# Both products of a scan step ahead of both scans, through two PSUM banks, with the attention's transposes in one bank

## What is computed

```python
# state-space layer, 256 inner channels, 16 states each
xz = einsum('blc,ec->ble', xn, W_in); xi, z = split(xz, 2)
xc = silu(conv4(xi)); dt, Bm, Cm = split(einsum('bld,ed->ble', xc, W_x))
delta = softplus(einsum('blr,dr->bld', dt, W_dt) + b_dt)
dA = exp(d_t[:, :, None] * A)
hst = hst * dA + (d_t * u_t)[:, :, None] * B_t[:, None, :]
y_t = einsum('bdn,bn->bd', hst, C_t)
out = einsum('bld,cd->blc', (y + xc * Dp) * silu(z), W_out) + x
# attention
energy = einsum('bci,bcj->bij', q, k)
out = gamma * einsum('bcj,bij->bci', v, softmax(energy)) + x
# second attention: energies of theta and phi, values x, then conv_w and batch norm, + x
```

## Time and profile before

| | |
|---|---|
| median of 3 runs | 5648.49 us (5642.84 to 5652.95) |
| the profiled execution's own time | 5654.98 us |
| its span, first to last instruction | 5653.2 us |
| mean granted clock of TensorE | 0.955 |
| VectorE busy | 5067.2 us, 90% |
| GpSimd busy | 4724.3 us, 84% |
| TensorE busy (matmuls) | 4649.7 us, 82% |
| ScalarE busy | 3709.2 us, 66% |

### The profile page before, as it was taken

One profiled execution on the slowest core, in us unless ns is written; L12 is line 12 of the kernel. 1 busy time (PEld: TensorE's weight loads), 2 busy tenths in 40 slices (PEclk: granted clock), 3 DMA queues, 4 the chain that ended last, 5 costly groups with the idle time before them and its releaser, 6 DMA issues.

```text
span 5653.2 us, 61917 instructions
## 1 busy us (share of the span) xinstructions
PE 4649.7 (82%) x17331; PEld 2705.2 (48%) x17331; DVE 5067.2 (90%) x5978; ACT 3709.2 (66%) x6077; POOL 4724.3 (84%) x3342
## 2 busy tenths in 40 slices
PE   6568888888888888888888888888888888888871
PEld 6135554455445444545444455445445544554450
DVE  4699999999999999999999999999999999999933
ACT  3456677667766766676677667766666776677633
POOL 0698999999989889898989998989889899999910
PEclk9689999999999999999999999999999999999995
DMA  4456656655655565555556665665566566656517
GB/s 132 176 224 224 224 208 223 229 222 216 224 224 215 215 225 217 216 219 225 223 207 224 224 225 217 222 220 212 219 224 223 210 221 229 224 208 224 219 74 301
DMA packets 199100, 1216.87 MB, mean 215 GB/s; under 512 B 27881, under 2 KB 28657, under 8 KB 67697
## 3 DMA queue, kind: packets, MB, share of 16 engines
q1 hardware_dynamic: 194416, 1196.26, 57.4%
q10 hardware_dynamic: 4352, 16.78, 0.7%
HBM read 1158.43 MB, written 54.53 MB: 215 GB/s over the span
## 4 chain that ended last, share of the span: by engine, by line
PE 38%; DVE 22%; ACT 14%; issue 13%; POOL 10%; DMA 1%; DVEq 0%; SPq 0%; POOLq 0%; ACTq 0%
PE psA L814 13%; PE psE L814 11%; DVE hs L488 8%; DVE psD L484 7%; PE psT L814 7%; POOL pa L300 5%; PE psT L987 4%; ACT da L680 4%; ACT p L726 3%; DVE nm L513 3%; PE psY L814 2%; POOL pa L306 2%; POOL pa L310 1%; ACT L649 1%; ACT pt L690 1%
## 5 line engine op out<-in xcount | busy, mean ns | idle before, releaser
L300 POOL TENSOR_TENSOR pa<-hs,rows_all 128x1024 f32<-128x1024 f32 x1024 | 2412.8, 2356 | 396.8 <-DVE hs L488 396.5
L680 ACT ACTIVATE da<-delta,neg_a 128x512 f32<-128x512 f32 x2048 | 1382.1, 719 | 288.3 <-DVE hs L488 276.2
L484 DVE TENSOR_TENSOR psD<-rows_all,psU 128x512 f32<-128x512 f32 x2048 | 1416.5, 692 | 84.7 <-POOL hlast L304 6.3
L306 POOL TENSOR_TENSOR pa<-pa 128x512 f32<-128x512 f32 x1024 | 1317.1, 1286 | 40.2
L488 DVE TENSOR_TENSOR_SCAN hs<-da,hlast,psD 128x512 f32<-128x512 f32 x1024 | 1310.9, 1280 | 36.3
L488 DVE TENSOR_TENSOR_SCAN hs<-da,psD 128x512 f32<-128x512 f32 x1024 | 1249.4, 1220 | 35.2
L814 PE MATMUL psA<-pt,va 128*128 128x256 f32 x4096 | 989.5, 391 | 71.2 <-DVE x L531 43.7
L814 PEld LDWEIGHTS psA<-pt,va 128*128 128x128 f32 x4096 | 770.0, 194 | 295.5 <-DVE x L531 77.1
L513 DVE TENSOR_REDUCE nm<-psE 128x1 f32<-128x1024 f32 x512 | 620.1, 1211 | 201.1 <-PE psE L814 198.8
L726 ACT ACTIVATE p<-psE,nm 128x1024 f32<-128x1024 f32 x512 | 571.5, 1116 | 316.8 <-DVE nm L513 316.7
L690 ACT ACTIVATE pt<-psT 128x512 f32<-128x512 f32 x1024 | 555.5, 596 | 304.4 <-PE psT L987 301.0
(11 more groups left out here) (186 smaller groups left out, 5017.6 us busy)
## 6 DMA issues: line engine op xcount, KB each, us to landing
rows_all<-bc_scratch SPq DMA_DIRECT2D x1024, 1024.0 KB, 4.7
xin<-x SPq DMA_DIRECT2D x40, 512.0 KB, 7.7
xres<-x SPq DMA_DIRECT2D x64, 256.0 KB, 6.1
x_scratch<-x SPq DMA_DIRECT2D x32, 512.0 KB, 4.3
f_scratch<-fa SPq DMA_DIRECT2D x32, 512.0 KB, 6.8
xres<-x SPq DMA_DIRECT2D x8, 512.0 KB, 3.6
x1g<-x SPq DMA_DIRECT2D x8, 512.0 KB, 3.7
fa<-x SPq DMA_DIRECT2D x8, 512.0 KB, 3.7
```

The lines of the kernel that those rows point to most:

```text
L300: pool.tensor_tensor(pa[:, k % PROD, :, :], hs[:, sl, :, :], rows_all[:, slot, 2:4, :], ALU.mult).then_inc(S["prod"], 1)
L306: pool.tensor_tensor(pa[:, k % PROD, 0, :], pa[:, k % PROD, 0, :], pa[:, k % PROD, 1, :], ALU.add).then_inc(S["pair"], 1)
L484: dve.tensor_tensor(psD[:, :], rows_all[:, slot, j, :], psU[:, :], ALU.mult).then_inc(S["dbu_ok"], 1)
L680: act.activation(da[:, k % 2, j, :], delta[:, h, cols(ch)], ACT.Exp, scale=neg_a[:, h, 2 * q + j:2 * q + j + 1]).then_inc(S["da_ok"], 1)
```

## The change

psD gets a second bank. psA is no longer a bank of its own: it is bank 1 of psT. What shared psT has to move:

- DVE: `scans` is split into `spread_inputs` (both products of a step, each into its own bank) and `scan_state` (one scan). A step is now: product 0, product 1, (xn), scan 0, small items, scan 1, row maximum, attended. The psU copy (`inputs`) is made in the step before it is needed, between the two scans. The waits for POOL (`prod`, `hlast_ok`) stand ahead of the first scan and not of the first product.
- PE and ACT: both halves of a tile's transposes go through bank 0 of psT; a half waits until ACT has copied the half before it. `ORDER` puts other work between the halves where there is some. The keys go through psE. The variance and both step sizes go through bank 0 (one after the other), the two gates are separate words in the order 1, 0, inner1 stands a step earlier, and the residual's first product is a word of its own.

```diff
-        psD = ps("psD", [128, CH])
+        psD = ps("psD", [128, 2, CH])
         psT = ps("psT", [128, 2, CH])
-        psA = ps("psA", [128, CH])
+        psA = psT[:, 1, :]
...
-        AT_C, AT_N, AT_X, AT_Z, AT_B, AT_P = 0, 3, (5, 7), 9, 10, 11
+        AT_C, AT_N, AT_X, AT_Z, AT_B, AT_P = 0, 3, (5, 6), 9, 10, 11
...
+                def inputs(b, k):
+                    ch, h = divmod(k // PAIRS, NH)
+                    wait(dve, "du_ok", b, k // PAIRS + 1)
+                    wait(dve, "dbu_ok", b, 2 * k)
+                    dve.tensor_copy(psU[:, :], du[:, h, cols(ch)]).then_inc(S["u_ok"], 1)
+
+                def spread_inputs(b, k):
+                    slot = k % RING
+                    if k % PAIRS == 0:
+                        wait(dve, "u_ok", b, k // PAIRS + 1)
+                    at(dve, f"rl{slot}", (b * (STEPS // RING) + k // RING + 1) * 16)
+                    for j in range(2):
+                        wait(dve, "h_ok", b, 2 * (k - 1) + j + 1)
+                        dve.tensor_tensor(psD[:, j, :], rows_all[:, slot, j, :], psU[:, :], ALU.mult
+                                          ).then_inc(S["dbu_ok"], 1)
+
+                def scan_state(b, k, j):
...
+                    sl = k % 2
                     if j == 0:
-                        at(dve, f"rl{slot}", (b * (STEPS // RING) + k // RING + 1) * 16)
                         wait(dve, "prod", b, k - 1)
                         wait(dve, "hlast_ok", b, min(k - 1, NS))
-                    wait(dve, "h_ok", b, 2 * k + j)
-                    dve.tensor_tensor(psD[:, :], rows_all[:, slot, j, :], psU[:, :], ALU.mult).then_inc(S["dbu_ok"], 1)
                     wait(dve, "dbu_ok", b, 2 * k + j + 1)
                     wait(dve, "da_ok", b, 2 * k + j + 1)
...
                             if scan:
-                                scans(b, k, 0)
+                                spread_inputs(b, k)
                             if front_of and r == AT_N:
                                 normed(*front_of)
+                            if scan:
+                                scan_state(b, k, 0)
+                            if scan and k % PAIRS == PAIRS - 1 and (k < STEPS - 1 or more):
+                                inputs(*((b, k + 1) if k < STEPS - 1 else (b + 1, 0)))
...
                             if scan:
-                                scans(b, k, 1)
+                                scan_state(b, k, 1)
...
-                    for q in range(2):
-                        wait(pe, "pt_ok", a, 2 * (i - 1) + q + 1)
-                        for j in range(4):
-                            last = pe.transpose(psT[:, q, 128 * j:128 * j + 128],
-                                                p[:, i % 2, (4 * q + j) * 128:(4 * q + j + 1) * 128], ident[:, :])
-                        last.then_inc(S["turn"], 1)
+                    wait(pe, "pt_ok", a, 2 * i + q)
+                    for j in range(4):
+                        last = pe.transpose(psT[:, 0, 128 * j:128 * j + 128],
+                                            p[:, i % 2, (4 * q + j) * 128:(4 * q + j + 1) * 128], ident[:, :])
+                    last.then_inc(S["turn"], 1)
...
                 ORDER = [
                     "centre add variance",
-                    "add energy turn weigh0",
-                    "weigh1 turn add residual",
+                    "add energy turn0 weigh0 turn1",
+                    "weigh1 turn0 resx turn1 residual",
                     "weigh0 weigh1 add",
                     "inner0 add",
-                    "project add",
-                    "project_values add inner1",
+                    "query inner1 add",
+                    "key values",
                     "energy add",
-                    "skip0 energy turn add",
-                    "gates add energy_next",
-                    "rows turn add",
-                    "add energy steps weigh0",
-                    "turn weigh1 turn_more skip1 add energy_next",
+                    "skip0 energy turn0 gates1 turn1",
+                    "gates0 add energy_next",
+                    "rows turn0 turn1",
+                    "add energy steps0 weigh0",
+                    "steps1 weigh1 turn0 skip1 turn1 more0 energy_next more1",
                     "add",
-                    "weigh0 energy turn add",
-                    "turn weigh1 add energy_next",
+                    "weigh0 energy turn0 turn1",
+                    "turn0 weigh1 turn1 add energy_next",
                 ]
```

188 lines of the change are left out of this document (101 added, 87 removed).

## The result

The changed kernel takes 5775.2 us (5770.4 to 5786.1), the kernel before 5653.0 us (5642.8 to 5656.4) beside it on the same chip: ratio 1.0222 (1.0208 to 1.0236). The forecast was 5680 us. The direction and the range hold; the size does not: +122 us where +31 were forecast. The profiled execution took 5770.44 us.

What follows compares the result with a forecast made beforehand. Rings through ScalarE and TensorE were taken to set the pace, with VectorE last only in 17 to 23. Per image +0.12 us plus +0.6 for clock: 31 x 0.72 + 8 = 30 us on 5648.5, near 5680 us; range 5540 to 5790.

Steps and rivals of the forecast that it cites:

- VectorE's part: With two psD banks no product or scan depends on its direct neighbour, 0.12 us saved each; -1.95 us per image.
- 17 to 23: From the row maximum of step 17 to that of 23: VectorE last, 29.25 to 27.3 us, -1.95 per image.
- The rival without a saving: VectorE's starts don't move, so 17 to 23 keeps 29.25 + 0.6 us; 5740 us, chance 0.10.
- 23 to 27: Row maximum 23 to 27: same ring as 7 to 11, but already holding a half-clock piece; 0 us per image.
- 29 to 33: Row maximum 29 to 33 (next image's step 1): as 13 to 17 with a shorter VectorE tail; +0.65 us per image.
- 13 to 17: Row maximum 13 to 17: step 12's last half behind energy 13 delays exp 13 and rb; +0.97 us per image.
- 33 to 7: Row maximum 33 (next image's step 1) to 7: TensorE full, saved stall offset by tile 7's halves; 0 us.
- 7 to 11: Row maximum 7 to 11: ScalarE held 0.79 us more by tile 1's copies; 20.7 against 20.25 us, +0.45 per image.
- 11 to 13: Row maximum 11 to 13: half turn and second skip less, one bare hop more; 0 us, VectorE only waits longer.
- The clock: One more half-clock TensorE piece in each second image, at 1.4 us; +0.6 us per image with the smaller ones.
- The clock's rival: Two more half-clock pieces per image on TensorE's path, 1.4 us each; 5745 us, up to 5790; chance 0.14.
- The end without scans: Last two images' attention, a ring of ScalarE and TensorE alone: 8 us more taken, at most 12.6.

## Why the forecast was right in direction and too small

**What bounds the kernel.** Right. The rings through ScalarE and TensorE set the pace, VectorE's saving went mostly into waits (L521's idle 627.5 us, forecast above 300), and TensorE's share of the chain rose from 38% to 54%.

**VectorE's part.** Right in its size per pair and in its place: the pairs of products take 1.28 us and the pairs of scans 2.32, so 0.6 and 1.14 apart, and 17 to 23 went to 27.15 (27.3 forecast, -2.09 against -1.95). The rival without a saving falls: old and new order in the same kernel differ by 198 us. The Trainium skill (VectorE: DVE Perf Modes, "The DRAIN you can't avoid") says that a semaphore between neighbours costs nothing extra. These runs don't bear that out for a wait on the direct neighbour: the earlier trace rows and the pairs above put it at 0.12 us. But "this is the only long stretch where VectorE is last" was true of the kernel before alone. With the longer rings of the one bank, the old order would also have lost in 23 to 27 (22.13 to 20.94, though 21.21 in the images without a piece there), 29 to 33, 13 to 17 and 33 to 7. I had set the saving against rings of before, not against the rings that the change makes.

**7 to 11.** Right in the ring: exp 8 at +6.81 (6.67 forecast), exp 10 another 10.88 later (10.82), 20.97 in all (20.7). Against the 20.25 us of the earlier trace rows that is +0.71; that the means differ by 0.36 only, near the 0.45 forecast, is luck, since 6 of 24 images before had a piece at half clock here and none has one now. 23 to 27, the same ring, was put at 0: at full clock it is +0.25, and on the mean -0.39, because its pieces are gone too.

**11 to 13: the step that failed.** "One half turn and the second skip less, one bare hop more ahead of energy 13; I take 0." It measured +0.95, and in 27 to 29, which has the same work, +1.03: together 1.98 of the 2.88 us per image that the forecast is short, and 2.27 of the 3.2 that the rings at full clock are above the forecast's +0.12. In the sum one bare hop more was set equal to a half turn less and a skip less. But the skip had not left the stretch: TensorE's rows above have it at 3061.52 still, between the halves, and `skip1` stands in both lists of words. (The rows of the new order in "The change" begin behind it, so it only looks gone there.) Without the skip in the sum the hop, 0.98 us more than a half without one, is set against 0.44 alone: 0.54 us, near the 0.58 of the rows. The earlier trace rows has this stretch with TensorE busy for 10.33 of 10.33 us, so a hop there could hide behind nothing; "VectorE only waits longer" names the engine that is not last. The other 0.39 us, the step product cut in two, I had priced at nothing, as moved but not added.

**13 to 17.** Right in the ring: exp 13 came at +3.61 (3.65) and the values product at +3.62 (3.45), which is what counts here, and without the piece at half clock maximum 14 came at +7.37 (7.2) and 14 to 16 took 9.41 (9.3), in all +1.26 against +0.97. The rest of the +2.74 is the piece, there in 25 of 29 images, which makes 13 to 14 longer by 1.48 on the mean. The late half was rightly taken for the place of a loss, but not for one that is worth much by itself: moved ahead of the energy it won 15 us.

**29 to 33 and 33 to 7.** 29 to 30 is 6.96 us, +1.07. At full clock the whole stretch is +0.99 against +0.65. The pieces in 30 to 32 cost 0.53 us on the mean now and 0.29 before. 33 to 7 is unchanged, as forecast.

**The clock.** The forecast's term of +0.6 was too large, not too small. It counted new pieces alone, and the ones behind maximum 13 did come, but those of 7 to 11 and 23 to 27 went: 1.74 us per image before, 2.01 after, +0.3. The clock's rival (5745 to 5790) had the time right by luck: it wanted two more pieces on TensorE's path on top of rings at +0.12, and measured are rings at +3.33 and +0.3 of clock.

**The sum.** At full clock the rings give +3.33 us per image where the forecast had +0.12. Of the 3.2 missing, 2.27 are in 11 to 13 and 27 to 29, 0.34 in 29 to 33, 0.29 in 13 to 17, 0.26 in 7 to 11, 0.25 in 23 to 27; 17 to 23 and 33 to 7 give 0.2 back, and the clock 0.3. The end without scans was sized well: from the first maximum of the last attention to the last instruction it is 9.2 us more, 8 forecast. The Trainium skill (Perfetto Trace Analysis, "Matmuls") speaks against one bank for groups that could rotate; the run with the one bank alone agrees, with 471 us.

**What stays open.** What decides whether a piece at half clock comes behind a given idle stretch. The runs exclude that the gap in front of it decides alone: in the same kernel 2.36 us were followed by it in 25 images and not in 4. 1.78 us were followed by it in every image of one kernel and mostly not in the other, but there the gap before that one differed too. The gain of moving the late half therefore can't be split fully into hop and clock. And the +0.33 by which 27 to 29 rose more than 11 to 13 at full clock was not followed up; it took 10.00 us in the two images before.

## What to carry to other kernels

When one change frees an engine and narrows a buffer of two others, price each against the rings as they will be, in a kernel with only one of the two if it can be had: here they were +320 and -198 us, and a sum of small terms hid both. A buffer cut from two banks to one cost less where other work stood between its two uses and nothing urgent stood behind the second use in the consumer's queue; look first at the stretch whose bottleneck is busy 100%, since there every hop counts in full. The order of the consumer's queue is worth a look of its own: an exponential ahead of a copy gave 211 us, more than VectorE's new order (198). And before a loss is put down to the clock, compare stretches that ran at the same level in both kernels: the pieces were the most visible thing in the new profile and made 0.3 of 3.6 us per image.
